# Weight ternarization of a sandwich kernel, issued inside the attention loop instead of behind it

## The chip, the cores and the metric

The kernel runs on one Trainium2 chip, on all 8 of its cores. Each core computes one of the 8 sequences (2048 tokens of 1024 channels) with the whole of the weights, and no core exchanges data with another. The time is that of the device in microseconds (us) for the slowest core.

## What is computed

Two layers, each an attention and a feed-forward part with layer norms around them. Only layer 0 matters here. Cut to what is near the change:

```python
# layer 0, attention
scores = where(tril, (q @ k.T) / sqrt(d), -inf); A = softmax(scores)
out = A @ C - diag(A) * (w2 * v_next)        # C: v convolved over 3 tokens
x = x + layernorm(out)
# layer 0, feed-forward
def _ternary(w):
    scale = maximum(mean(abs(w)), 1e-8)
    return clip(round(w / scale), -1, 1)     # in value
h   = gelu(layernorm(x) @ _ternary(W1).T + b1)
out = h @ _ternary(W2).T + b2
x = x + layernorm(out)
# layer 1 (decay attention, mixture of attention heads and experts): untouched
```

W1 is 4096 x 1024 and W2 1024 x 4096 in fp32, 16 MB each. The ternary weights need a mean over the whole matrix before the first element can be rounded, so each matrix is read twice. They depend on nothing that the attention computes.

## The kernel before

Everything is in one function, `build`. Every engine has one program in order: `kb.q` appends to SyncE's (SP), which issues DMAs, `kb.g` to GpSimd's (POOL), `kb.t` to TensorE's (PE), `kb.v` to VectorE's (DVE), `kb.s` to ScalarE's (ACT). The order of the calls in Python is therefore the order on each engine, and an engine that waits for a semaphore holds up all that was appended to it later. Semaphores `ct`, `cv`, `cs`, `cg` count the work done on PE, DVE, ACT and POOL. A token is a pair of semaphore and count; `wait(engine, *tokens)` waits for each.

The stages around the change, in order:

- **Attention of layer 0** (L515 to L681), 16 query tiles of 128 rows, tile i against the i+1 key tiles before it. Per tile: DVE copies the scores from four PSUM banks to `S_sb` (L565), POOL masks the diagonal block (L572), DVE takes the row maximum (L581), ACT does the exponential into `P_sb` (L587). PE is given the scores of the next tile, `emit_scores(i + 1)` (L547, call at L595), and only behind them the transposes of `P_sb` (L605), which DVE copies to `AT_sb` in one or two batches (L614). DVE then builds `B_sb` and `Dw_sb` (L622, L633), PE transposes `Dw_sb` (L300), DVE copies it (L308), PE forms the output product in `ps_o` (L650, L654), DVE copies that to `q_fm` (L670) and, with POOL, takes the layer norm's sums (`lnb.stats`, L199 to L246). Behind the loop stand `rstd_batch` (Ln and Exp on ACT, L256 and L263) and 16 times `apply` (DVE, L276 to L288).
- **B0, the ternarization** (L684 to L832). Both matrices go by in 32 batches (`batches`) of 128 x 2048 fp32, 1 MB each, through two slots of the buffer `tw`. Pass 1: SP loads a batch (L721) once the slot's last reader is done (`red_tok`), ACT takes the absolute value with a running sum into `asums` (L728). Then a short chain on DVE and PE turns `asums` into the thresholds `taus` (L739 to L782). Pass 2: SP loads the batch again (L804), DVE compares twice (`thr` L811, `wtb` L818), SP stores `wtb` as bf16 to the scratch `w1t_sc` or `w2t_sc` in HBM (L826). The two comparisons and the store share one `thr` and one `wtb`. In SP's program the load of batch k+1 stands behind the store of batch k, which waits for that batch's `wtb`.
- `kb.barrier()` for all engines and DMAs, then a second one without the DMAs.
- **B1** (L840 on): SP loads rows of x (L855), DVE adds the attention's output (L861), layer norm, transposes. Then the feed-forward part of layer 0 reads the ternary weights by transposing DMAs (L919 and w2tb).

Of the kernel before, what the change touches and what calls it, by code (L numbers as in the profile page):

```python
# [6 lines left out]
F32 = mybir.dt.float32  # L7
BF16 = mybir.dt.bfloat16
# [5 lines left out]
D = 1024  # L14
# [62 lines left out]
def wait(eng, *toks):  # L77
    for tk in toks:
        if tk is None:
            continue  # L80
        h, v = tk
        if v > 0:
            eng.wait_ge(h, v)
# [230 lines left out]
def build(debug=(), phases="ABCD"):  # L314
# [194 lines left out]
    kb.flush_dbg()  # L509
    kb.barrier()  # L510

    def outln_ap(i):
        return bass.AP(q_fm, 128 * i, [[q_fm.shape[1], 128], [T, ND], [1, 128]])

    with ExitStack() as pha:  # L515
# [42 lines left out]
        for i in range(NT):  # L558
# [34 lines left out]

            if i + 1 < NT:
                pend = emit_scores(i + 1)  # L595

            at_toks = []
            for bg in range((i + 8) // 8):
# [69 lines left out]
            def _(v, i=i, w=otok):  # L668
# [4 lines left out]

            stok = lnb.stats(outln_ap(i), i, [out_ps_free, rtok],
                             f_ap=ssum[:, 1:2], prev=stok)
        rtok_b = lnb.rstd_batch(0, 16, [stok])
        aptok = None
        for i in range(NT):
# [3 lines left out]
        kb.dbg("outln_q", q_fm[:], a3_done)  # L682
    kb.flush_dbg()

    if "B" in phases:
        NW = 4096 * D
        reg1_free = qkv_done
        NW = 4096 * D
        asums = kb.sbuf("asums", [128, 32], F32)
        taus = kb.sbuf("taus", [128, 4], F32)  # L690
        tot_sb = kb.sbuf("tot_sb", [1, 2], F32)
        ones_f = kb.sbuf("ones_f", [1, 128], F32)
        ones_c = kb.sbuf("ones_c", [128, 1], F32)

        def _(v):
            v.memset(ones_f[:], 1.0)
            cv.inc(v.memset(ones_c[:], 1.0))
        kb.v(_)
        vof = cv.tok()

        W1r = inp["L0_ffn_W1"].rearrange("(c p) d -> p c d", p=128)
        W2r = inp["L0_ffn_W2"].rearrange("(c p) d -> p c d", p=128)
        tw = kb.at("tw", [128, 2 * 2048], F32, REG1)
        thr = kb.at("thr", [128, 2048], BF16, REG1 + 16384)
        wtb = kb.at("wtb", [128, 2048], BF16, REG1 + 20480)
        dts = [kb.dsem("t0"), kb.dsem("t1")]
        red_tok = {0: None, 1: None}
        batches = []
        for b in range(16):
            batches.append((W1r[:, 2 * b:2 * b + 2, :], b))  # L710
        for b in range(16):
            c, h = b // 2, b % 2
            batches.append((W2r[:, c:c + 1, h * 2048:(h + 1) * 2048], 16 + b))
        for src_ap, col in batches:
            slot = col % 2
            twa = tw[:, slot * 2048:(slot + 1) * 2048]

            def _(sync, src_ap=src_ap, twa=twa, w=red_tok[slot], ds=dts[slot],
                  w2=(reg1_free if col < 2 else None)):
                wait(sync, w, w2)  # L720
                ds.inc(sync.dma_start(out=twa.rearrange("p (c d) -> p c d",  # L721
                                                        c=src_ap.shape[1]), in_=src_ap))
            kb.q(_)
            ltok = dts[slot].tok()

            def _(s, twa=twa, col=col, ltok=ltok, pv=red_tok[1 - slot]):
                wait(s, ltok, pv)
                cs.inc(s.activation(thr[:], twa, AF.Abs,  # L728
                                    accum_out=asums[:, col:col + 1]))
            kb.s(_)  # L730
            red_tok[slot] = cs.tok()
        red_all = cs.tok()

        scope_b0 = ExitStack()
        ps_sc = kb.psum("ps_sc", [128, 2], F32, scope_b0)
        for m, (c0, c1) in enumerate(((0, 16), (16, 32))):
            def _(v, m=m, c0=c0, c1=c1, w=red_all):
                wait(v, w)
                cv.inc(v.tensor_reduce(sm[:, 9 + m:10 + m], asums[:, c0:c1], AX.X, ALU.add))  # L739
            kb.v(_)  # L740
        tsum_tok = cv.tok()

        def _(t, w=tsum_tok, w2=vof):
            wait(t, w, w2)
            t.matmul(ps_sc[0:1, 0:1], sm[:, 9:10], ones_c[:], start=True, stop=True)
            ct.inc(t.matmul(ps_sc[0:1, 1:2], sm[:, 10:11], ones_c[:], start=True, stop=True))
        kb.t(_)
        ttot = ct.tok()

        def _(v, w=ttot):  # L750
            wait(v, w)
            cv.inc(v.tensor_scalar_mul(tot_sb[0:1, 0:2], ps_sc[0:1, 0:2], 1.0 / NW))
        kb.v(_)
        vv1 = cv.tok()

        def _(v, w=vv1):
            wait(v, w)
            cv.inc(v.tensor_scalar(tot_sb[0:1, 0:2], tot_sb[0:1, 0:2], 1e-8, 0.5,
                                   ALU.max, ALU.mult))
        kb.v(_)  # L760
        vv2 = cv.tok()

        ps_tau = kb.psum("ps_tau", [128, 2], F32, scope_b0)

        def _(t, w=vv2):
            wait(t, w)
            ct.inc(t.matmul(ps_tau[:, 0:2], ones_f[:], tot_sb[0:1, 0:2],
                            start=True, stop=True))
        kb.t(_)
        tbc = ct.tok()  # L770

        def _(v, w=tbc):
            wait(v, w)
            v.tensor_copy(taus[:, 0:1], ps_tau[:, 0:1])
            v.tensor_copy(taus[:, 2:3], ps_tau[:, 1:2])
            cv.inc(v.tensor_scalar_mul(taus[:, 1:2], ps_tau[:, 0:1], -1.0))
        kb.v(_)
        vt_ = cv.tok()

        def _(v, w=vt_):  # L780
            wait(v, w)
            cv.inc(v.tensor_scalar_mul(taus[:, 3:4], ps_tau[:, 1:2], -1.0))  # L782
        kb.v(_)
        tau_tok = cv.tok()

        W1s = w1t_sc.rearrange("(c p) d -> p c d", p=128)
        W2s = w2t_sc.rearrange("(c p) d -> p c d", p=128)
        dst_sem = kb.dsem("ts")
        st_tok = None
        vthr_tok = None  # L790
        for src_ap, col in batches:
            m = 0 if col < 16 else 1
            slot = col % 2
            twa = tw[:, slot * 2048:(slot + 1) * 2048]
            if col < 16:
                dst = W1s[:, 2 * col:2 * col + 2, :]
            else:
                c, h = (col - 16) // 2, (col - 16) % 2
                dst = W2s[:, c:c + 1, h * 2048:(h + 1) * 2048]

            def _(sync, src_ap=src_ap, twa=twa, w=red_tok[slot], ds=dts[slot],
                  vt=vthr_tok):
                wait(sync, w, vt)
                ds.inc(sync.dma_start(out=twa.rearrange("p (c d) -> p c d",  # L804
                                                        c=src_ap.shape[1]), in_=src_ap))
            kb.q(_)
            ltok = dts[slot].tok()

            def _(v, twa=twa, m=m, ltok=ltok, w=st_tok):
                wait(v, ltok, tau_tok, w)  # L810
                cv.inc(v.tensor_scalar(thr[:], twa, taus[:, 2 * m + 1:2 * m + 2], 1.0,  # L811
                                       ALU.is_ge, ALU.subtract))
            kb.v(_)
            th1 = cv.tok()

            def _(v, twa=twa, m=m, th1=th1):
                wait(v, th1)
                cv.inc(v.scalar_tensor_tensor(wtb[:], twa, taus[:, 2 * m:2 * m + 1],  # L818
                                              thr[:], ALU.is_gt, ALU.add))
            kb.v(_)  # L820
            vthr_tok = cv.tok()
            red_tok[slot] = vthr_tok

            def _(sync, dst=dst, w=vthr_tok):
                wait(sync, w)
                dst_sem.inc(sync.dma_start(  # L826
                    out=dst, in_=wtb[:].rearrange("p (c d) -> p c d", c=dst.shape[1])))
            kb.q(_)
            st_tok = dst_sem.tok()
        kb.barrier()  # L830

        scope_b0.close()  # L832


    kb.barrier(dma=False)


    if "B" in phases:
        scope_b1 = ExitStack()
# [71 lines left out]
        for grp in range(4):  # L911
            for p in range(8):
                slot = p % 2

                def _(sync, p=p, slot=slot, w=w1slot_tok[slot], ds=dw1[slot],
                      w2=(st_tok if (grp == 0 and p < 2) else None)):
                    wait(sync, w, w2)
                    for dc in range(8):
                        ds.inc(sync.dma_start(  # L919
                            out=w1tb[:, slot * 4096 + dc * 512:slot * 4096 + (dc + 1) * 512],  # L920
                            in_=w1t_sc[p * 512:(p + 1) * 512, dc * 128:(dc + 1) * 128],
                            transpose=True))
# [3 lines left out]
                for fpr in range(2):  # L926
# [20 lines left out]
                    kb.t(_)  # L947
                    mtok = ct.tok()

                    def _(s, pb=pb, p=p, fpr=fpr, mtok=mtok, hf=hg_free):  # L950
                        wait(s, mtok, hf)
                        fc0 = 4 * p + 2 * fpr
                        cs.inc(s.activation(h_g[:, fc0 * 512:(fc0 + 2) * 512], pb[:],  # L953
                                            AF.Gelu))
# [8 lines left out]
            for pair in range(2):  # L963
                for fc in range(32):
                    slot = fc % 2
                    wslice = w2tb[:, slot * 1024:(slot + 1) * 1024]
                    def _(sync, fc=fc, wslice=wslice, w=w2slot_tok[slot], ds=dw2[slot],
                          w2=(st_tok if (grp == 0 and pair == 0 and fc < 2) else None)):
                        wait(sync, w, w2)
                        ds.inc(sync.dma_start(out=wslice,  # L970
                                              in_=w2t_sc[:, fc * 128:(fc + 1) * 128],
# [1391 lines left out]
```

How the kernel before makes its waits and increments, by code:

```python
    def inc(self, ins, n=None):  # L67
        n = self.step if n is None else n
        ins.then_inc(self.h, n)
        self.val += n
        return (self.h, self.val)
# [5 lines left out]
def wait(eng, *toks):  # L77
    for tk in toks:
        if tk is None:
            continue
        h, v = tk
        if v > 0:
            eng.wait_ge(h, v)
```

## Time and profile before

| | |
|---|---|
| time, median of 2 runs | 6173.97 us (6172.5 to 6175.44) |
| time of the profiled execution | 6228.01 us |
| its span, core 1 (slowest) | 6226.5 us |
| spans of the 8 cores | 6137.2 to 6226.5 us |
| PE, DVE, ACT, POOL busy | 2947.0, 1919.9, 854.7, 335.0 us |
| chain that ended last | PE 41%, DVE 21%, DMA 14%, issue 9%, ACT 6% |

The profile is of one execution, on its slowest core, core 1; all times below are from that core, counted from its first instruction. The kernel is a sequence of stages with different limits, so that shares over the whole span say little about one stage. In the span, the attention of layer 0 lies at 545 to 953 us, B0 behind it up to 1436 us, B1 up to about 1600 us, and the feed-forward part of layer 0 up to about 2900 us.

### The profile page before, as it was taken

What the parts mean: (1) busy time and instruction counts of PE and PEld (TensorE: products, weight loads), DVE (VectorE), ACT (ScalarE), POOL (GpSimd) and SP (SyncE); (2) the same over time, 40 slices, a digit from 0 to 9 for tenths busy, and PEclk for the clock granted to TensorE, in tenths of its full rate; (3) what the DMA queues carried; (4) which work ended last, traced back from release to release, by engine and by line L of the source; (5) the groups of instructions that cost most, each with busy time, mean ns of one, the idle gap of its engine ahead of it and who ended that gap; (6) DMA issues with size and microseconds to landing.
All of it is one profiled execution on the core that took longest, in us unless ns stands there. A gap on an engine that the chain in (4) does not pass through costs nothing.

```text
span 6226.5 us, 41618 instructions; the slowest of 8 cores (6137.2 to 6226.5 us)
## 1 busy us (share of the span) xinstructions
PE 2947.0 (47%) x11532; PEld 1153.8 (19%) x11532; DVE 1919.9 (31%) x4762; ACT 854.7 (14%) x828; POOL 335.0 (5%) x234
## 2 busy tenths in 40 slices
PE   0672550000666666651342021663432399988970
PEld 0221220000212121210210010221111133333330
DVE  4225441335100000003555642333344222222224
ACT  0000116000204040311000001001100222222220
POOL 2000000001000000001101300000010000000001
PEclk9995775555757575765665555765575678899975
DMA  1100005442343434340001004000000311111102
GB/s 27 27 14 14 0 1 198 153 142 88 68 92 72 95 73 97 73 80 7 0 1 55 0 1 41 0 0 0 14 0 1 54 28 28 28 28 28 28 4 105
DMA packets 494200, 274.39 MB, mean 44 GB/s; under 512 B 439680, under 2 KB 447904, under 8 KB 489888
## 3 DMA queue, kind: packets, MB, share of 16 engines
q1 hardware_dynamic: 438784, 218.18, 13.8%
q0 software_dynamic: 55200, 53.56, 5.6%
q8 instruction: 108, 1.77, 0.1%
q14 instruction: 108, 0.88, 0.1%
HBM read 190.97 MB, written 33.55 MB: 36 GB/s over the span
## 4 chain that ended last, share of the span: by engine, by line
PE 41%; DVE 21%; DMA 14%; issue 9%; ACT 6%; POOL 5%; SPq 2%; DVEq 1%; POOLq 0%; ACTq 0%
DMA w2tb<-w2t_sc 7%; PE ps_m5a L2268 4%; POOL sq_scr L208 4%; DMA tw<-L_ffn_W 4%; PE ps_m5b L2268 4%; PE ps_i5a L2229 4%; PE ps_o L983 4%; PE ps_i5b L2229 4%; PE ps_qkv L441 3%; DVE lnst L214 3%; PE ps_h L937 3%; SPq L919 2%; PE ps_o L650 1%; PE ps_q L1929 1%; PE ps_s L547 1%
## 5 line engine op out<-in xcount | busy, mean ns | idle before, releaser
L983 PE MATMUL ps_o<-w2tb,h_g 128*128 128x512 bf16 x1024 | 439.9, 583 | 277.3 <-DMA w2tb<-w2t_sc 245.8
L937 PE MATMUL ps_h<-act_fm,w1tb 128*128 128x512 bf16 x1024 | 277.9, 420 | 151.5 <-ACT h_g L953 81.1
L2268 PE MATMUL ps_m5a<-w2b,scaled 128*128 128x512 bf16 x1024 | 290.4, 435 | 112.3 <-DVE scaled L2251 112.3
L2241 ACT ACT_TABLE_LOAD x128 | 164.2, 1283 | 843.7 <-PE ps_i5a L2229 755.6
L2268 PE MATMUL ps_m5b<-w2b,scaled 128*128 128x512 bf16 x1024 | 274.8, 417 | 0.0
L2229 PE MATMUL ps_i5a<-act_fm,w1b 128*128 128x512 bf16 x1024 | 248.8, 399 | 28.1 <-DMA w2b<-L_ffn_w 28.1
L208 POOL TENSOR_TENSOR sq_scr<-X 128x1024 f32<-128x1024 f32 x96 | 181.6, 1892 | 1249.6 <-DVE X L861 547.5
L2229 PE MATMUL ps_i5b<-act_fm,w1b 128*128 128x512 bf16 x1024 | 246.9, 397 | 0.0
L2251 DVE TENSOR_TENSOR scaled<-scaled,rw2b_eg 128x512 bf16<-128x512 bf16 x256 | 97.4, 422 | 482.1 <-ACT scaled L2241 482.1
L300 PE MATMUL ps_tr<-idbf,tmb 128*128 128x128 bf16 x128 | 16.2, 305 | 473.9 <-DVE tmb L288 473.9
L1018 DVE TENSOR_REDUCE smB<-out2g 128x1 f32<-128x1024 bf16 x16 | 19.5, 1220 | 711.8 <-ACT out2g L1006 711.8
L256 ACT ACT_TABLE_LOAD x10 | 12.8, 1283 | 1537.5 <-DVE lnst L246 1537.5
L441 PE MATMUL ps_qkv<-n_fm,wbuf 128*128 128x512 bf16 x768 | 184.8, 384 | 78.9 <-DVE q_fm L455 22.7
L983 PEld LDWEIGHTS ps_o<-w2tb,h_g 128*128 128x128 bf16 x1024 | 108.9, 123 | 606.0 <-issue 597.8
L1929 PE MATMUL ps_q<-n1e,qp_b 128*128 128x512 bf16 x256 | 129.0, 504 | 183.5 <-DVE n1e L1914 129.7
L214 DVE TENSOR_REDUCE lnst<-sq_scr 128x1 f32<-128x1024 f32 x144 | 175.7, 1220 | 124.7 <-POOL sq_scr L208 124.7
L300 PE MATMUL ps_trF<-idbf,tmd 128*128 128x128 bf16 x256 | 32.3, 305 | 328.6 <-DVE tmd L288 328.6
L2268 PEld LDWEIGHTS ps_m5a<-w2b,scaled 128*128 128x128 bf16 x1024 | 107.3, 107 | 270.0 <-issue 204.1
L2282 DVE TENSOR_TENSOR X<-X,ps_m5a 128x512 f32<-128x512 f32 x128 | 88.0, 688 | 216.4 <-PE ps_m5a L2268 216.4
L937 PEld LDWEIGHTS ps_h<-act_fm,w1tb 128*128 128x128 bf16 x1024 | 96.8, 104 | 298.1 <-issue 232.7
L547 PE MATMUL ps_s<-k_fm,q_fm 128*128 128x512 bf16 (+3 forms) x320 | 92.1, 464 | 99.0 <-DVE S_sb L565 96.9
L2282 DVE TENSOR_TENSOR X<-X,ps_m5b 128x512 f32<-128x512 f32 x128 | 88.1, 688 | 164.6 <-PE ps_m5b L2268 164.6
(311 smaller groups left out, 4128.4 us busy)
## 6 DMA issues: line engine op xcount, KB each, us to landing
tw<-L_ffn_W SPq DMA_DIRECT2D x64, 1024.0 KB, 5.7
w1b<-L_ffn_w POOLq DMA_DIRECT2D x8, 2048.0 KB, 13.7
w2b<-L_ffn_w POOLq DMA_DIRECT2D x8, 2048.0 KB, 22.7
w1t_sc<-wtb SPq DMA_DIRECT2D x16, 512.0 KB, 3.2
w2t_sc<-wtb SPq DMA_DIRECT2D x16, 512.0 KB, 3.4
xt<-L_attn_x SPq DMA_DIRECT2D x16, 512.0 KB, 3.3
x_sc<-X SPq DMA_DIRECT2D x16, 512.0 KB, 2.6
xt<-x_sc SPq DMA_DIRECT2D x16, 512.0 KB, 4.0
```

The source lines that it names most:

```text
L208: cg.inc(g.tensor_tensor(sq, src_ap, src_ap, ALU.mult))
L214: cv.inc(v.tensor_reduce(va, sq, ax, ALU.add))
L441: t.matmul(pb[:], wbuf[:, slot * 4096 + kc * 512 + fc4 * 128: slot * 4096 + kc * 512 + (fc4 + 1) * 128], n1_fm[:, kc * T + tg * 512: kc * ...
L547: ins = t.matmul(ps_s[bk][:, 0:w1c - w0c], q_fm[:, kc * T + i * 128: kc * T + (i + 1) * 128], k_fm[:, kc * T + w0c: kc * T + w1c], start=( ...
L919: ds.inc(sync.dma_start(out=w1tb[:, slot * 4096 + dc * 512:slot * 4096 + (dc + 1) * 512], in_=w1t_sc[p * 512:(p + 1) * 512, dc * 128:(dc + ...
L937: t.matmul(pb[:, half * 512:(half + 1) * 512], w1tb[:, slot * 4096 + kc * 512 + fl * 128: slot * 4096 + kc * 512 + (fl + 1) * 128], act_fm ...
L983: ins = t.matmul(ps_o2[u][:, half * 512:(half + 1) * 512], h_g[:, fc * 512 + sub * 128:fc * 512 + (sub + 1) * 128], wslice[:, half * 512:( ...
L1929: t.matmul(ps_q3[:], qp_b[:, fl:fl + 128], n1e[:, cc * 512:(cc + 1) * 512], start=st_, stop=sp)
L2229: ins = t.matmul(ps_i5[bk][:, half * 512:(half + 1) * 512], w1b[:, slot * 8192 + cc * 1024 + ic * 128: slot * 8192 + cc * 1024 + (ic + 1) ...
L2241: cs.inc(s.activation(scaled[:, ipr * 1024:(ipr + 1) * 1024], ps_i5[bk][:], AF.Gelu))
L2268: ins = t.matmul(ps_m5[bk][:], scaled[:, ic * 512 + u * 128:ic * 512 + (u + 1) * 128], w2b[:, slot * 8192 + ic * 1024 + half * 512: slot * ...
L2282: cv.inc(v.tensor_add(dd, dd, ps_m5[bk][:]))
```

## The change

The ternarization is cut into steps, closures in a list `b0_steps`: 32 of pass 1, one `tau_step`, 32 of pass 2, 65 in all. The list is made ahead of the attention. In the attention's loop, right behind `emit_scores(i + 1)` and ahead of the transposes of tile i, two steps are taken off and issued in tile 0 and five in each later tile; what is left would be issued behind the loop, ahead of `rstd_batch`. So tiles 0 to 6 get the 32 steps of pass 1, tile 7 gets `tau_step` and four steps of pass 2, tiles 8 to 12 five each, and tile 13 the last three. A step issues on the same engines as before: SP and ACT for pass 1, SP and DVE for pass 2, DVE and PE for tau. The two small PSUM tiles of tau become one of four columns, so that it fits beside the attention's seven banks. The load of pass 2 no longer waits for `vthr_tok`, the batch before; its place in SP's program is the same. The barrier with DMAs behind B0 is gone, the one without stays. The first readers of the scratch and the first writer of the region that `tw` shares with `h_g` wait for the last store and the last comparison.

```diff
+    b0_steps = []
+    b0_state = {}
...
+        def mk_pass1(src_ap, col):
+            def step():
...
+                def _(sync, w=b0_state["red_tok"][slot], ds=dts[slot],
+                      w2=(reg1_free if col < 2 else None)):
+                    wait(sync, w, w2)
+                    ds.inc(sync.dma_start(out=twa.rearrange("p (c d) -> p c d",
+                                                            c=src_ap.shape[1]),
+                                          in_=src_ap))
+                kb.q(_)
+                ltok = dts[slot].tok()
+
+                def _(s, ltok=ltok, pv=b0_state["red_tok"][1 - slot]):
+                    wait(s, ltok, pv)
+                    cs.inc(s.activation(thr[:], twa, AF.Abs,
+                                        accum_out=asums[:, col:col + 1]))
+                kb.s(_)
+                b0_state["red_tok"][slot] = cs.tok()
+            return step
+
+        def tau_step():
+            red_all = cs.tok()
...
+        def mk_pass2(src_ap, col):
+            def step():
...
+                def _(sync, w=b0_state["red_tok"][slot], ds=dts[slot]):
+                    wait(sync, w)
...
+                kb.q(_)
+                ltok = dts[slot].tok()
+
+                def _(v, m=m, ltok=ltok, w=b0_state["st_tok"]):
+                    wait(v, ltok, b0_state["tau_tok"], w)
+                    cv.inc(v.tensor_scalar(thr[:], twa, taus[:, 2 * m + 1:2 * m + 2],
+                                           1.0, ALU.is_ge, ALU.subtract))
+                kb.v(_)
...
+                def _(sync, dst=dst, w=vthr):
+                    wait(sync, w)
+                    dst_sem.inc(sync.dma_start(
+                        out=dst, in_=wtb[:].rearrange("p (c d) -> p c d",
+                                                      c=dst.shape[1])))
+                kb.q(_)
+                b0_state["st_tok"] = dst_sem.tok()
+            return step
+
+        for src_ap, col in batches[:32]:
+            b0_steps.append(mk_pass1(src_ap, col))
+        b0_steps.append(tau_step)
+        for src_ap, col in batches:
+            b0_steps.append(mk_pass2(src_ap, col))
...
             if i + 1 < NT:
                 pend = emit_scores(i + 1)
+            for _k in range(5 if i else 2):
+                if b0_steps:
+                    b0_steps.pop(0)()
...
+        while b0_steps:
+            b0_steps.pop(0)()
         rtok_b = lnb.rstd_batch(0, 16, [stok])
...
+    kb.barrier(dma=False)
     if "B" in phases:
-        NW = 4096 * D
...
-        for src_ap, col in batches:
-            slot = col % 2
...
-        kb.barrier()
-
-        scope_b0.close()
-
-
-    kb.barrier(dma=False)
-
+        scope_b0ps.close()
...
-                    def _(s, pb=pb, p=p, fpr=fpr, mtok=mtok, hf=hg_free):
-                        wait(s, mtok, hf)
+                    def _(s, pb=pb, p=p, fpr=fpr, mtok=mtok, hf=hg_free,
+                          bf=(b0_state.get("st_tok") if grp == 0 and p < 2 else None),
+                          bv=(b0_state.get("vthr_tok") if grp == 0 and p < 2 else None)):
+                        wait(s, mtok, hf, bf, bv)
```

## Rows read from the trace of the kernel before

**Rows 1.** Stages: from:to, length, busy us (instructions) by engine, granted clock, DMA.

```profile
core 1: us, PE busy (x) PEld busy (x) DVE busy (x) ACT busy (x) POOL busy (x), PEclk, DMA share, GB/s
688.00:953.00 265.00, 149.54 (x638) 64.97 (x638) 108.61 (x306) 26.56 (x27) 19.66 (x18) 0.73 0.00 1
957.80:1095.60 137.80, 0.00 (x0) 0.00 (x0) 13.13 (x47) 103.86 (x96) 0.00 (x0) 0.50 0.70 236
1095.60:1435.70 340.10, 0.79 (x6) 0.66 (x6) 117.43 (x72) 0.00 (x0) 0.00 (x0) 0.50 0.43 145
```

**Rows 2.** Tile tw: ns min/median/max, first and last start us; DVE's idle; landing.

```profile
L728 ACT ACTIVATE thr<-tw x32: 1909/1909/1910, 957.8 to 1093.6; 128x2048 bf16<-128x2048 f32 x32
L811 DVE TENSOR_SCALAR thr<-tw,taus x32: 1285/1286/1289, 1098.5 to 1429.4; 128x2048 bf16<-128x2048 f32 x32
...
  DMA tw<-L_ffn_W: 214.9, 31
...
DMA to landing us min/median/max: 4.8/5.7/6.9
```

**Rows 3.** Timeline behind tile 15: start us, us, engine, line, what [idle before].

```profile
953.09 0.16 DVE L246 TENSOR_TENSOR lnst<-lnst 128x1 f32<-128x1 f32 x1
...
956.53 1.28 ACT L728 ACT_TABLE_LOAD   x1
...
957.16 0.55 DVE L288 TENSOR_SCALAR q_fm<-q_fm,lnst 128x1024 bf16<-128x1024 bf16 x1
...
974.92 0.55 DVE L288 TENSOR_SCALAR q_fm<-q_fm,lnst 128x1024 bf16<-128x1024 bf16 x1
```

**Rows 4.** Timeline: tau, the first two batches of pass 2, B1's first load.

```profile
1096.23 0.19 PE L745 MATMUL ps_sc<-ones_c,sm 128*1 128x1 f32 x2 [149.04 <-DVE sm L739]
...
1098.45 1.29 DVE L811 TENSOR_SCALAR thr<-tw,taus 128x2048 bf16<-128x2048 f32 x1
...
1102.28 0.40 SPq L826 DMA_DIRECT2D w1t_sc<-wtb  x1
1102.83 0.37 SPq L804 DMA_DIRECT2D tw<-L_ffn_W  x1
1108.98 1.28 DVE L811 TENSOR_SCALAR thr<-tw,taus 128x2048 bf16<-128x2048 f32 x1 [6.78 <-DMA tw<-L_ffn_W]
1110.38 2.35 DVE L818 SCALAR_TENSOR_TENSOR wtb<-tw,taus,thr 128x2048 bf16<-128x2048 f32 x1
...
1436.10 34.03 SPq L855 DMA_DIRECT2D xt<-L_attn_x  x8
```

**Rows 5.** Timeline of ACT: exponentials of tiles 2, 4, 6, with ACT's idle ahead.

```profile
582.48 1.28 ACT L587 ACT_TABLE_LOAD   x1 [16.47 <-DVE sm L581]
...
622.99 1.28 ACT L587 ACT_TABLE_LOAD   x1 [19.01 <-DVE sm L581]
...
666.85 1.28 ACT L587 ACT_TABLE_LOAD   x1 [19.46 <-DVE sm L581]
```

**Rows 6.** Timeline of DVE: first copies to AT_sb in tiles 7, 8, 13.

```profile
695.58 0.69 DVE L614 COPY AT_sb<-ps_at 128x1024 bf16<-128x1024 bf16 x1 [4.59 <-PE ps_at L605]
...
720.17 0.69 DVE L614 COPY AT_sb<-ps_at 128x1024 bf16<-128x1024 bf16 x1 [4.35 <-PE ps_at L605]
...
865.07 0.69 DVE L614 COPY AT_sb<-ps_at 128x1024 bf16<-128x1024 bf16 x1 [5.64 <-PE ps_at L605]
```

**Rows 7.** Timeline of PE: first half of the output product, tiles 13 and 15.

```profile
871.62 4.55 PE L650 MATMUL ps_o<-C_tm,AT_sb 128*128 128x512 bf16 x14 [1.61 <-DVE ssum L664]
...
936.80 6.50 PE L650 MATMUL ps_o<-C_tm,AT_sb 128*128 128x512 bf16 x16 [1.61 <-DVE ssum L664]
```

**Rows 8.** The page's DMA issues: KB each, us to landing.

```profile
w2b<-L_ffn_w POOLq DMA_DIRECT2D x8, 2048.0 KB, 22.7
...
wbuf<-L_attn_W_qkv POOLq DMA_DIRECT2D x6, 1024.0 KB, 8.6
```

More of the change, by code:

```diff
@@ L683, in build @@
     kb.flush_dbg()
+    kb.barrier(dma=False)
     if "B" in phases:
-        NW = 4096 * D
[L687 to L710, printed above, removed]
@@ L711, in build @@
-        for b in range(16):
-            c, h = b // 2, b % 2
-            batches.append((W2r[:, c:c + 1, h * 2048:(h + 1) * 2048], 16 + b))
-        for src_ap, col in batches:
-            slot = col % 2
[L716 to L829, printed above, removed]
@@ L915, in _ @@
                 def _(sync, p=p, slot=slot, w=w1slot_tok[slot], ds=dw1[slot],
-                      w2=(st_tok if (grp == 0 and p < 2) else None)):
+                      w2=(b0_state.get("st_tok") if (grp == 0 and p < 2) else None)):
                     wait(sync, w, w2)
@@ L967, in _ @@
                     def _(sync, fc=fc, wslice=wslice, w=w2slot_tok[slot], ds=dw2[slot],
-                          w2=(st_tok if (grp == 0 and pair == 0 and fc < 2) else None)):
+                          w2=(b0_state.get("st_tok") if (grp == 0 and pair == 0 and fc < 2) else None)):
                         wait(sync, w, w2)
```

97 lines of the change are left out of this document (added).

## The prediction, written before the changed kernel was run

> **What bounds the kernel now.** I read the page's chain of work that ended last first, to learn that no one engine bounds the whole, then cut the span into stages. The reader is to see two things in [rows 1]. B0 is 137.8 us of pass 1 and 340.1 us of pass 2, and PE does nothing in them (6 instructions in 478 us). The attention ahead of it has no DMA traffic (1 GB/s) and ACT works 26.56 us in 265, so work of the one could lie beside work of the other. Next I read the buffer tw: in pass 2, DVE is idle for 214.9 us in 31 waits, each for a load [rows 2]. The timeline shows why [rows 4]: the store of a batch goes out at 1102.28, the next load right behind it at 1102.83, and DVE begins at 1108.98 after 6.78 us idle. The load is never early, since it stands behind the store on SP, and the store needs the comparisons. So one batch of pass 2 costs a period: (1429.4 - 1098.5) / 31 = 10.67 us [rows 2], of which DVE works 1.29 + 2.35, some 3.7 us with the gap between. Last I read the timeline of the attention: its tiles are one serial chain over DVE, POOL, ACT and PE, in which DVE's idle time is short pieces. This decides the sum: what is put into DVE's program there is hidden only as far as DVE was idle at that very place.
>
> **What is removed.** From the end of tile 15's sums (953.25) to B1's first load (1436.10) is 482.9 us [rows 3, 4]. Of that stretch rstd and the 16 applies stay. They were hidden under pass 1; now their cover is gone, and they end at 975.47, 22.2 us after 953.25 [rows 3]. With 0.3 us for the barrier, 22.5 us stay and 460 us go. B1's first load comes just after the barrier in both kernels, so that its landing costs the same.
>
> **Pass 1 in tiles 0 to 6.** SP's loads wait for nothing but their slots, and SP has nothing else in this stage. On ACT a batch is 103.86 / 32 = 3.25 us busy [rows 1], 3.4 with the gap, and behind the batches stands the next tile's exponential, for which all of the chain waits. Two batches of five have their loads in place when the exponential ends; the others follow at the pace of landing (4.8 to 6.9 us, median 5.7 [rows 2]): starts at about 0, 3.4, 9, 12.5 and 17.5 to 18.5, end at 21 to 22. Between two exponentials ACT was idle 16.47, 19.01 and 19.46 us ahead of tiles 2, 4 and 6 [rows 5]. Against 21 this is late by 4.5, 2.0 and 1.5 us; tiles 3 and 5 I take between, 3 and 2, tile 7 at nothing: 13 us. The bounds: ACT's work alone, 5 x 3.4 = 17, makes it 1 us; the pace of pass 1 of before, (1093.6 - 957.8) / 31 = 4.38 a batch [rows 2] or 22 for five, makes 18. The two batches of tile 0 cost nothing under the idle time ahead of tile 1.
>
> **Tau, in tile 7.** PE reaches it behind the scores of tile 8, which end about 0.7 us before the copy at 695.58 [rows 6]; the chain from its first matmul to pass 2 takes 1098.45 - 1096.23 = 2.2 us [rows 4]. Pass 2 thus begins about 697.1. Its four batches take 3.7 (its load came in long ago) + 3 x 10.67 = 35.7 us, to 732.8: the copy to AT_sb comes 37.3 us late, and PE's transposes are behind tau as well.
>
> **Pass 2 in tiles 8 to 13.** The first load of each tile stands behind the last store of the tile before and is long in place. The other four wait as before, with their order on SP unchanged; the dropped wait for vthr_tok gains nothing, since SP's program holds the load back anyway. DVE is held for 3.7 + 4 x 10.67 = 46.4 us, in tile 13 for 3.7 + 2 x 10.67 = 25.0. Behind it on DVE stands the copy to AT_sb, and for this wait PE's second transposes and the output product, then DVE's own sums and the next tile's scores. What hides is the idle time ahead of that copy, 4.35 to 5.64 us [rows 6]; I take 5 (exponential, scores and first transposes run on under the block). So 5 x 41.4 + 20 = 227 us. With tile 7, pass 2 costs 264 us of its former 340. That is 25 waits for a load where there were 31, and six tiles' gaps of 5 us. A bound from below: nothing of it can take less than the comparisons alone, 32 x 3.7 - 35 = 83 us; from above, with nothing hidden, 300. SP's order speaks for the middle.
>
> **The clock.** PE will be idle some 40 us in each of seven tiles. Now the first half of the output product takes 325 ns a matmul in tile 13 (4.55 / 14), behind recent scores, and 406 in tile 15 (6.50 / 16), which has no scores ahead [rows 7]: the 1.2 GHz level, where 512 columns are 0.43 us, held longer. Like tile 15, tiles 7 to 13 lose 14 x 0.08 = 1.1 us each, 8 in all, and 2 for colder transposes: 10 us. Bounds: nothing, and all 84 matmuls of the second halves at 0.43 in place of 0.21, 18 + 6 = 24 us. The Trainium skill, "TensorE: Matmul & The Clock Gate", section "Part 1: The HAM clock gate (the "warmup" mystery)", says that the slow clock is the default and activity releases it, which speaks against a change that makes PE pause. The trace agrees with the rule in kind (325 against 406 ns). If it were to bite on all of the output products, my sum would be 14 us smaller.
>
> One more rule would speak against mixing Abs and Exp on ACT. In the trace the switch is free: a table load of 1.28 us stands ahead of each batch anyway, and the one at 956.53 comes directly behind an Exp [rows 3]. The Trainium skill, "ScalarE: Activation LUTs", section "What ACT_TABLE_LOAD costs", adds a drain of 1.38 us for a switch to another set; as an estimate that would take 2 x 1.38 us in each of five tiles, 14 us more. The row decides against it.
>
> **Sum.** 460 - 13 - 264 - 10 = 173 us less. Of the profiled execution's 6228 (span 6226.5, 1.5 around it) this leaves 6055. The profiled execution is 54 us above the median of the runs; the stages concerned scarcely hold more than their share of that (attention and B0 are 14% of the span, 8 us), so I carry the difference over whole: 6174 - 173 = 6001 us, 2.8% less.
>
> **The rivals.**
> (a) Dearer loads, within 2%. All eight cores drift apart, and a load may meet others' traffic or work here. It decides from 50 us more (2% of 6174 is 123), 2 us for each of the 25 loads that DVE waits for. At 3 us each, 75 us in all: 6076. Against it: 64 loads of 1 MB landed in 4.8 to 6.9 us with all cores at it, at up to 236 GB/s a core [rows 1, 2], and the new stage asks for less per time. A lesser hiding or a colder PE (10 + 14) push the same way. Chance 0.17.
> (b) Slower. The one mechanism: loads placed in the attention take as long as those that other parts of the kernel show, 8.6 us for 1 MB in wbuf, up to 22.7 for 2 MB in w2b [rows 8], and DVE's block grows with each. Break-even is at 173 / 25 = 7 us more a load, 13 to landing; over 2% slower from 12 us more, about 18. At 22.7 to landing, 17 more: 6001 + 425 = 6426. Those are of POOL's queue with a conversion of type on the way, these are of SP's; nothing of the trace puts SP's above 6.9. Chance 0.04, most of it for slower by over 2%.
> (c) More is hidden. If loads of pass 2 did come ahead of DVE, the block of a tile is 5 x 3.7 = 18.5 less 5 hidden, and the whole 83 + 2 for tau in place of 264: 180 us more saved, 5821. For it: the wait on vthr_tok is gone, and two slots are there. Against it: SP's program order. Chance 0.05.
> (d) The change does not do what it says: the steps only move the wait, and with the applies bare nothing is won. It would need pass 1 to cost on ACT what it did alone, 138 us in place of 13: 6001 + 125 = 6126, within 2%. The idle times of 16 to 19 us a tile speak against it. Chance 0.03.
>
> **How the numbers follow.** The forecast has the remaining 0.71; its own range, from pass 1 (1 to 18), the clock (0 to 24), the hiding (4 to 7 us a tile) and the carry-over to the median, is 5965 to 6040. The range that holds 8 in 10 takes in the nearer part of (a) as well: 5950 to 6070. Faster by over 2% means below 6050: forecast and (c), 0.76; (a) and (d) are within 2%, with part of (b): 0.21; slower 0.03. About 2% is what a measurement of this kernel can tell from no change.
>
> **What would show it.** In the changed kernel's timeline: pass 1's Abs between the exponentials of tiles 0 to 6, and tiles 1 to 5 longer by 1 to 5 us; in tiles 8 to 12 five pairs of comparisons on DVE at 10.5 to 11 us from one to the next, the first without a wait, and each tile some 42 us longer than before; DVE's idle time for loads in pass 2 near 25 x 7 = 175 us in place of 214.9; PE's output products there beginning at over 400 ns a matmul; from the last tile's sums to B1's first load 22 to 23 us; all later stages as long as before. The prediction is wrong if the pairs follow each other at 4 us (c) or at 13 and more (a, b), if exponentials come over 10 us late in tiles 1 to 6 (d), or if a later stage changes its length.

## The result and the profile after

The changed kernel takes 5976.97 to 6020.49 us; its ratio to the kernel before, taken from runs on the same chips, is 0.968 with a 95% interval of 0.962 to 0.974. That is 3.2% less, some 198 us of 6174, where 2.8% and 6001 us were forecast.

The profiled execution of the changed kernel fell on a run in which all eight cores had a lower mean clock (0.677 to 0.687 of full speed, against 0.70 in the runs of 5977 to 5987 us), so its span of 6100.7 us is not to be set against 6226.5. What can be compared is the stretch that the change touches, from the first copy of scores in the attention's tile 0 to B1's first load. On core 1 it is 889.8 us before (546.30 to 1436.10) and 709.4 after (549.07 to 1258.49), 180.4 less; the medians over the eight cores are 888.8 and 710.2.

The stages after on core 1, to be read against [rows 1]: from:to, length, busy us (instructions) of each engine, granted clock, DMA share, GB/s.

```profile
549.10:705.00 155.90, 68.26 (x251) 27.59 (x252) 66.60 (x216) 120.63 (x118) 15.58 (x15) 0.64 0.66 222
705.00:1146.40 441.40, 106.84 (x448) 46.81 (x446) 187.27 (x271) 19.10 (x21) 13.11 (x12) 0.60 0.33 111
1146.40:1236.00 89.60, 44.89 (x189) 19.78 (x189) 35.45 (x106) 6.65 (x6) 6.26 (x5) 0.67 0.02 6
1236.00:1258.50 22.50, 0.00 (x0) 0.00 (x0) 13.95 (x49) 3.09 (x4) 0.00 (x0) 0.50 0.00 0
1258.50:6100.70 4842.20, 2554.04 (x9518) 973.18 (x9518) 1409.05 (x3614) 702.17 (x676) 260.19 (x170) 0.66 0.18 37
```

The first row is tiles 0 to 6 with pass 1: ACT is busy 120.63 of 155.90 us, and the DMA queues run at 222 GB/s beside PE's and DVE's own work. The second, tiles 7 to 13 with pass 2, is the long one: in 441 us DVE is busy 187. The largest part of the rest stands in the answer for the tile tw (min/median/max ns, first and last start; idle us, times), beside [rows 2]:

```profile
L563 ACT ACTIVATE thr<-tw x32: 1909/1910/1911, 556.7 to 701.4; 128x2048 bf16<-128x2048 f32 x32
L645 DVE TENSOR_SCALAR thr<-tw,taus x32: 1276/1286/1287, 710.1 to 1142.8; 128x2048 bf16<-128x2048 f32 x32
...
  DMA tw<-L_ffn_W: 173.1, 25
...
DMA to landing us min/median/max: 4.7/5.8/9.7
```

25 waits for a load, 173.1 us, where the forecast had 25 and near 175. The timeline of tile 8 shows each of them (start us, us, engine, line, what [idle before]), as [rows 4] did before:

```profile
768.98 1.28 DVE L645 TENSOR_SCALAR thr<-tw,taus 128x2048 bf16<-128x2048 f32 x1
...
772.79 0.38 SPq L661 DMA_DIRECT2D w1t_sc<-wtb  x1
773.27 0.42 SPq L637 DMA_DIRECT2D tw<-L_ffn_W  x1
779.09 1.28 DVE L645 TENSOR_SCALAR thr<-tw,taus 128x2048 bf16<-128x2048 f32 x1 [6.37 <-DMA tw<-L_ffn_W]
...
810.81 1.29 DVE L645 TENSOR_SCALAR thr<-tw,taus 128x2048 bf16<-128x2048 f32 x1 [7.05 <-DMA tw<-L_ffn_W]
...
814.47 0.68 DVE L780 COPY AT_sb<-ps_at 128x1024 bf16<-128x1024 bf16 x1
```

The first pair has its load in place, the other four wait 6.4 to 7.1 us, since the load goes out behind the store. The copy to AT_sb, which waited 4.35 us for PE in [rows 6], now waits for nothing and comes 49.1 us after the tile's first copy of scores instead of 8.1.

### The profile page after: what moved, and what is told of

Same layout as the page of the kernel before. It is cut to its first block, busy times and chain, and to the rows that moved or that the text cites. A ratio compares the mean times of both kernels' runs of the same rounds, so it can differ in the third digit from the quotient of the medians.

```text
span 6100.7 us, 41540 instructions; the slowest of 8 cores (6032.4 to 6100.7 us)
## 1 busy us (share of the span) xinstructions
PE 3021.5 (50%) x11532; PEld 1170.2 (19%) x11532; DVE 1918.7 (31%) x4762; ACT 854.7 (14%) x828; POOL 335.0 (5%) x234
## 3 DMA queue, kind: packets, MB, share of 16 engines
q1 hardware_dynamic: 438784, 218.18, 13.9%
## 4 chain that ended last, share of the span: by engine, by line
PE 42%; DVE 22%; DMA 13%; issue 9%; ACT 6%; POOL 5%; SPq 2%; DVEq 1%; POOLq 0%; ACTq 0%
DMA w2tb<-w2t_sc 7%; PE ps_m5a L2289 5%; POOL sq_scr L208 4%; PE ps_m5b L2289 4%; PE ps_i5a L2250 4%; PE ps_i5b L2250 4%; PE ps_o L1004 4%; DMA tw<-L_ffn_W 3%; PE ps_qkv L441 3%; PE ps_h L956 3%; DVE lnst L214 3%; SPq L938 2%; PE ps_q L1950 1%; DVE n1e L1935 1%; PE ps_o L816 1%
## 5 line engine op out<-in xcount | busy, mean ns | idle before, releaser
L956 PE MATMUL ps_h<-act_fm,w1tb 128*128 128x512 bf16 x1024 | 295.6, 441 | 142.5 <-ACT h_g L974 79.1
L2250 PE MATMUL ps_i5a<-act_fm,w1b 128*128 128x512 bf16 x1024 | 257.5, 410 | 22.9 <-DMA w2b<-L_ffn_w 22.9
L1039 DVE TENSOR_REDUCE smB<-out2g 128x1 f32<-128x1024 bf16 x16 | 19.5, 1220 | 727.9 <-ACT out2g L1027 727.9
L750 ACT ACT_TABLE_LOAD x16 | 20.5, 1283 | 924.8 <-DVE sm L744 924.7
L771 PE MATMUL ps_at<-idbf,P_sb 128*128 128x128 bf16 x136 | 13.8, 247 | 259.8 <-DVE AT_sb L780 233.0
## 6 DMA issues: line engine op xcount, KB each, us to landing
w1b<-L_ffn_w POOLq DMA_DIRECT2D x8, 2048.0 KB, 13.5
w2b<-L_ffn_w POOLq DMA_DIRECT2D x8, 2048.0 KB, 22.6
```

Source lines behind the costliest of these rows:

```text
L956: t.matmul(pb[:, half * 512:(half + 1) * 512], w1tb[:, slot * 4096 + kc * 512 + fl * 128: slot * 4096 + kc * 512 + (fl + 1) * 128], act_fm ...
L2250: ins = t.matmul(ps_i5[bk][:, half * 512:(half + 1) * 512], w1b[:, slot * 8192 + cc * 1024 + ic * 128: slot * 8192 + cc * 1024 + (ic + 1) ...
```

## The experiments

Each was run beside the kernel before on the same chip. The figure that decides is the stretch, as the median over the eight cores; the ratio stands beside it.

| kernel | attention begins | stretch | later stages | ratio to before (95%) |
|---|---|---|---|---|
| before | 547.3 | 888.8 | 4731.6 | 1 |
| changed | 548.0 | 710.2 | 4800.4 | 0.968 (0.962 to 0.974) |
| e1, pass 1 alone in the loop | 548.6 | 778.2 | 4712.4 | 0.982 (0.967 to 0.996) |
| e2, dropped wait put back | 548.5 | 711.2 | 4708.9 | 0.969 (0.960 to 0.979) |
| e3, loads ahead of the store | 548.5 | 625.5 | 4733.4 | 0.955 (0.948 to 0.963) |
| e4, and two wtb | 548.4 | 585.0 | 4754.2 | 0.950 (0.940 to 0.959) |
| e5, steps at two places | 548.0 | 505.9 | 4716.5 | 0.935 (0.930 to 0.941) |
| e6, ahead of the attention | 534.2 | 430.4 | 4735.9 | 0.923 (0.918 to 0.928) |
| e7, four banks alone | 477.2 | 715.4 | 4733.6 | 0.959 (0.954 to 0.963) |
| e9, spread over both | 497.9 | 431.2 | 4705.1 | 0.913 (0.897 to 0.930) |

**The theory**: DVE's program in order is the cost. Pass 2 costs its full period in the attention, less DVE's short idle time at that place, and the period is long because the load stands behind the store on SP. **The rivals**: pass 1 or a later stage is the gain; the dropped wait is; the landing or the queues' bandwidth sets the period, not the order.

**e1.** Pass 2 is taken out of the loop:

```diff
-                if b0_steps:
+                if len(b0_steps) > 33:
                     b0_steps.pop(0)()
```

> Only pass 1 is issued inside the attention's loop; tau and pass 2 stand behind the loop, ahead of rstd. Measured from the first score copy of tile 0 to B1's first load, the kernel before takes 889.8 us and the changed one 709.4. Theory (the sum of the prediction, step by step): pass 1 hides all but 10 us, tau and pass 2 cost 343 as before, rstd and the applies are bare: 407 + 10 + 343 + 22.5 = 782 us, 107 less than before, 73 more than the changed kernel; ratio to the kernel before about 0.983. Rival (pass 1 was the whole gain and moving pass 2 brought nothing): 710 us, ratio as the changed kernel's, 0.968. Rival (pass 1 hides poorly, pass 2 well): above 830 us, ratio over 0.99.

Measured 778.2 us, 4 off. So of the change's 179 us, pass 1 brings 111 and pass 2 68, though pass 2 is the longer by far (340 against 138). In ACT's idle time pass 1 is hidden but for some 10 us; what else is missing from 138 is mostly the 22.6 us of rstd and applies, which it used to cover. Pass 2 is mostly moved. The interval of its ratio is wide, 0.967 to 0.996; the stretch carries the verdict.

**e2.** The wait that the change drops is put back:

```diff
-                def _(sync, w=b0_state["red_tok"][slot], ds=dts[slot]):
-                    wait(sync, w)
+                def _(sync, w=b0_state["red_tok"][slot], ds=dts[slot],
+                      vt=b0_state["vthr_tok"]):
+                    wait(sync, w, vt)
```

> The changed kernel with the one dropped wait put back: SP's load of pass 2 waits again for the comparisons of the batch before. Theory (the order of SP's program holds the load back anyway, the dropped wait is worth nothing): no difference, 709 us for the stretch, 25 waits for loads of about 7 us, 173 us in all, ratio 0.968 to the kernel before. Rival (part of the gain came from this wait): pairs of comparisons further apart than the 10.5 of the changed kernel, stretch over 720 us.

711.2 against 710.2 us, and 25 waits, 176.9 us in all, on the profiled core. The wait was worth nothing: the load stands behind a store that waits for the same comparisons.

**e3.** The load of batch k+2 is issued behind the store of batch k, so that the one of k+1 is out before:

```diff
-                def _(sync, w=b0_state["red_tok"][slot], ds=dts[slot]):
-                    wait(sync, w)
...
+                if col == 0:
+                    load2(0)
+                    load2(1)
+                ltok = b0_state["ltok"][col]
...
                 b0_state["st_tok"] = dst_sem.tok()
+                if col + 2 < 32:
+                    load2(col + 2)
```

> The changed kernel with one thing moved: in pass 2 the load of batch k+2 is issued behind the store of batch k, so that the load of batch k+1 is always ahead of that store. Theory (SP's program order is what DVE pays for): DVE no longer waits for loads; the next limit is the one wtb, whose store has to land, 3.7 + about 3.8 us = 7.5 from one pair to the next; the block of five is 34 us in place of 46, and 25 x 3.1 = 78 us go: stretch 631 us, ratio to before about 0.956. Rival (the queues cannot carry load and store together, or the landing is what is slow): pairs stay 10 us or more apart, stretch above 690 us.

625.5 us, and the waits changed their name as expected. Timeline of DVE and SP, then the waits of the tile tw in this kernel:

```profile
799.84 1.28 DVE L656 TENSOR_SCALAR thr<-tw,taus 128x2048 bf16<-128x2048 f32 x1 [3.30 <-DMA w1t_sc<-wtb]
801.23 2.35 DVE L663 SCALAR_TENSOR_TENSOR wtb<-tw,taus,thr 128x2048 bf16<-128x2048 f32 x1
803.65 0.38 SPq L672 DMA_DIRECT2D w1t_sc<-wtb  x1
804.12 0.42 SPq L632 DMA_DIRECT2D tw<-L_ffn_W  x1
```

```profile
  DMA w1t_sc<-wtb: 44.1, 13
  DMA w2t_sc<-wtb: 43.3, 12
```

DVE waits for the store of its single wtb, 3.3 us each, and never for a load; the pairs are 7.1 us apart in place of the 10.3 to 10.8 above. Nothing but the order on SP was changed, and the loads land no faster (5.9 us at the median over pass 2, 6.0 in the changed kernel). So it was the order that put the load's landing into each period; a limit of bandwidth would have kept the pairs 10 us apart.

**e4.** The kernel of e3, and with two wtb, each with a semaphore for its store (a part of the edit, against the changed kernel):

```diff
-        wtb = kb.at("wtb", [128, 2048], BF16, REG1 + 20480)
-        dst_sem = kb.dsem("ts")
+        wtb2 = kb.at("wtb", [128, 2 * 2048], BF16, REG1 + 20480)
+        dsts = [kb.dsem("ts0"), kb.dsem("ts1")]
...
-                def _(v, m=m, th1=th1):
-                    wait(v, th1)
...
+                def _(v, m=m, th1=th1, w=b0_state["st"][slot]):
+                    wait(v, th1, w)
```

> As the one before, and with two wtb buffers, each with its store semaphore. Theory: the store's landing goes off the path too; of five batches in a tile two find their loads in place, the others come at the pace of landing, one load being issued each time a slot is read: the block is about 23 us, in tile 7 17 and in tile 13 13: some 149 us less than the changed kernel, stretch 560 us, ratio to before about 0.945. Rival (1 MB in and 0.5 MB out per batch saturate the queues): pairs 8 us or more apart, stretch above 620 us, no better than with the one buffer.

585.0 us: 125 less than the changed kernel, not the 149 expected, and between the theory's 560 and the rival's 620. The waits for loads are back, 54.7 us in 17, and the landings are longer than reckoned: from 697 us on, that is over pass 2, 7.6 us at the median and 10.9 at most, where the changed kernel has 6.0 and 8.0. In tile 9 a load issued at 809.59 is read at 817.52:

```profile
809.59 0.42 SPq L632 DMA_DIRECT2D tw<-L_ffn_W  x1
...
812.44 1.29 DVE L659 TENSOR_SCALAR thr<-tw,taus 128x2048 bf16<-128x2048 f32 x1 [3.39 <-DMA tw<-L_ffn_W]
...
817.52 1.28 DVE L659 TENSOR_SCALAR thr<-tw,taus 128x2048 bf16<-128x2048 f32 x1 [1.27 <-DMA tw<-L_ffn_W]
```

**e8.** To tell what made these landings long, e4 with the stores in the loop cut to 16 columns (`out=dst[:, 0:1, 0:16], in_=wtb[:, 0:16]`), and full stores, all from one buffer, behind the loop (so the ternary weights that it stores are not the right ones):

> As e4_two_out, but in the loop each store of pass 2 is cut to 16 columns, 4 KB; the stores in full stand behind the loop, all from one buffer, so the ternary weights of this kernel are wrong and about 80 us of stores come on top behind the loop. It tells why the block of five in e4_two_out is 25.6 us and not the 23 expected. Theory (loads are slowed by the 0.5 MB stores that run beside them): with the stores gone the loads that DVE waits for land in 5 to 5.7 us in place of 6.8 to 7.9, and the block is 22.5 to 23 us. Rival (two loads in flight slow each other, or the wait is SP's): landing and block stay as in e4_two_out, 25 us or more.

The waits for loads fall to 28.1 us in 15 from 54.7 in 17:

```profile
  DMA tw<-L_ffn_W: 28.1, 15
```

Over pass 2 its loads land in 5.2 us at the median and 6.3 at most, with two of them in flight as in e4, so two loads do not slow each other by much. From the first comparison to the copy to AT_sb, tiles 8 to 12 take 22.9 to 25.0 us on the profiled core, in e4 25.6 to 31.9; from tile 7's first copy of scores to that of tile 14 the medians over the cores are 321.5 and 344.0 us. The full stores beside the loads thus cost about 23 us, and e4 lay 25 above its 560: they are nearly all of its excess. (The stretch of e8, 565.5 us, holds the added stores behind the loop and is not set against the others.)

**e5.** In the kernel of e4, from tile 7 on one step stays at its place (in tile 7 tau and one) and three go behind the output product's matmuls:

```diff
-            for _k in range(5 if i else 2):
+            for _k in range(2 if i == 0 else (5 if i < 7 else (2 if i == 7 else 1))):
                 if b0_steps:
                     b0_steps.pop(0)()
...
             at_free = otok
+            for _k in range(0 if i < 7 else 3):
+                if b0_steps:
+                    b0_steps.pop(0)()
```

> As e4_two_out, but from tile 7 on four steps a tile at two places of DVE's program: one (in tile 7 tau and one) where the changed kernel has its steps, three behind the output product's matmuls, where DVE was idle 7.5 to 10.8 us for PE. Pass 2 then ends in tile 14. Theory (what is put into DVE's program is hidden only as far as DVE was idle at that place): the first step is covered, the three cost 12 us of comparisons and 3 of a wait for a load against 7.5 to 10.8, so 5 to 7 us a tile: the stretch from the first score copy to B1's first load goes from 585 (median of the cores, e4_two_out) to about 505 us, ratio to before about 0.937. Rival (the tiles are paced by the DMA queues, 6 MB a tile, wherever the steps stand): no better than 570.

505.9 us, for 505 expected. The same instructions, at other places of the same program, cost 79 us less. Not all of this is idle time used: the steps are also further apart, and DVE's waits for loads fall by 23 us (on core 5, from 54.7 in 17 to 31.8 in 8). Some 56 us are left for the place alone. The timeline of DVE in tile 11:

```profile
865.10 0.69 DVE L797 COPY AT_sb<-ps_at 128x1024 bf16<-128x1024 bf16 x1 [1.51 <-PE ps_at L788]
...
882.44 1.29 DVE L659 TENSOR_SCALAR thr<-tw,taus 128x2048 bf16<-128x2048 f32 x1 [3.75 <-DMA tw<-L_ffn_W]
883.90 2.35 DVE L666 SCALAR_TENSOR_TENSOR wtb<-tw,taus,thr 128x2048 bf16<-128x2048 f32 x1 [0.17 <-DVE thr L659]
886.24 1.21 DVE L856 CAST q_fm<-ps_o 128x1024 bf16<-128x1024 f32 x1
```

The copy to AT_sb still waits 1.51 us for PE, so the single step ahead of it cost nothing. The copy of the output comes 21.1 us behind it, 13.5 before: the three steps overrun PE's work by 7.7, half of it a wait for the third load.

**e6, e7.** The whole ternarization goes ahead of the attention, with its buffers where C_tm comes later: a step of pass 1 behind each tile of the first layer norm and beside the first groups of the projection, tau behind group 8, pass 2 over groups 9 to 95. The projection gets four PSUM banks in turn; e7 is the changed kernel with only this:

```diff
-                bk = fc4 % 2
-                pb = ps_q[bk]
                 for tg in range(4):
+                    bk = tg
+                    pb = ps_q[bk]
```

> The whole ternarization is moved ahead of the attention: pass 1 beside the first layer norm and the first groups of the q, k, v projection (SP and ACT idle there), tau and pass 2 beside the rest of the projection, one batch every 2.7 of its 96 groups, loads two ahead, two wtb, buffers in the region of C_tm. The projection gets four PSUM banks in turn in place of two. Theory: the attention and what follows go back to 407 + 23 = 430 us for the stretch (888.8 before, 710.2 changed, medians of the cores); the projection's DVE has 66 us of its own and gets 120 in 283, mostly hidden with four banks, so that the attention begins at 480 to 520 us (548 before); in all some 310 us less than the changed kernel, ratio to before about 0.915. Rival (DVE's blocks of 3.7 us stall PE in the projection in spite of the banks): the attention begins at 580 or later, ratio 0.93 or more.

> The changed kernel with the four banks in turn in the q, k, v projection alone, to tell their part in e6_early. Theory: PE no longer waits for DVE's copy between groups (68 us of idle time in the projection), the attention begins at about 480 us in place of 548, stretch unchanged at 710, ratio to before about 0.958. Rival: PE is bound by its own issue and weight loads, under 20 us are won.

The stretch is 430.4 us in e6, what the attention, rstd and applies took by themselves (407 + 23): everything of B0 is off it. e7 begins its attention at 477.2 us: the banks alone are worth 71 us, a gain that has nothing to do with the change. Against e7, e6 begins 57 us late, more than the 3 to 43 expected, and its ratio is 0.923 where 0.915 was expected.

**e9.** Tau behind group 20, 20 batches of pass 2 beside the projection, 12 one each in tiles 3 to 14:

> As e6_early, but tau stands behind group 20 of the projection's 96 instead of 8 (PE waited 24 us for pass 1 there), only 20 batches of pass 2 go beside the projection, one every 3.75 groups, and the last 12 go one each into the attention's tiles 3 to 14, at the changed kernel's place, with buffers in the region of n1_fm. Theory (e6_early lost its 57 us at the attention's start to tau and to loads: 1.5 MB a batch want 6.4 us and got 5.8): the attention begins at 485 to 495 us (534 in e6_early, 477 in e7_banks), the single steps in the tiles have their load in place and lie in DVE's idle time of 2.4 to 5.6 us, about 1 us each or less uncovered: stretch 430 to 442 us; some 40 us less than e6_early, ratio to before about 0.916. Rival (the projection loses by DVE's blocks themselves, 3.7 us against PE's two or three groups of lead): the start stays over 515 us.

Start 497.9, stretch 431.2 us, ratio 0.913: the lowest of all, though its interval is wide, 0.897 to 0.930, and holds that of e6. The profiles tell the two apart: start and stretch together are 929 us, some 35 less than in e6. The twelve single steps in the attention cost 1 us together against e6: a pair of 3.7 us lies in the idle time in front of AT_sb. The rival falls: the 20 batches beside the projection waited 1.0 us for loads in all, and none of PE's waits for DVE in it is over 0.7 us (tau apart). Still the start is 21 us behind e7's and 3 behind what was expected. Part of it is the projection's own first load: on core 1, PE begins the projection at 193.24, in e7 at 176.98. The timeline of e9 (core 1), then the landing of wbuf's six loads:

```profile
170.33 1.79 POOL L611 DMA_DIRECT2D wbuf<-L_attn_W_qkv  x2 [63.77 <-DVE n_fm L308]
...
193.24 3.57 PE L630 MATMUL ps_qkv<-n_fm,wbuf 128*128 128x512 bf16 x8 [25.07 <-DMA tw<-L_ffn_W]
```

```profile
DMA to landing us min/median/max: 8.2/18.4/29.5
```

PE waits 25.07 us, which the trace puts down to a load of tw; but its wait there is for wbuf, whose load went out at 170.33. In e7 the same wait is 13.9 us. With the ternarization's loads in flight, wbuf's take 18.4 us at the median (21.9 in e6) in place of the 8.6 of [rows 8]; they are POOL's and convert fp32 to bf16. e6's 57 us were followed only in part: on core 1 its projection begins at 187.27, 10 us behind e7's, and PE waited 19.5 us for DVE's copies in it, as the rival had it; the rest stays open.

## Why the prediction was right, point by point

Against the steps of the prediction, on core 1:

| step | forecast | measured |
|---|---|---|
| stretch removed, rstd and applies left | 482.9, 22.5 | 482.9, 22.6 |
| pass 1 in tiles 0 to 6 | 13 (1 to 18) | 10.3 |
| tau and four batches in tile 7 | 37.3 | 39.0 |
| pass 2 in tiles 8 to 13 | 227 | 225.0 |
| colder PE | 10 (0 to 24) | 5.3 |
| net | 173 | 180.4 |

**The bare applies.** From the end of tile 15's sums to B1's first load, the changed kernel's timeline, as [rows 3] before:

```profile
1235.93 0.16 DVE L246 TENSOR_TENSOR lnst<-lnst 128x1 f32<-128x1 f32 x1
...
1240.00 0.55 DVE L288 TENSOR_SCALAR q_fm<-q_fm,lnst 128x1024 bf16<-128x1024 bf16 x1
...
1258.49 0.80 SPq L874 DMA_DIRECT2D xt<-L_attn_x  x2
```

**Pass 1.** ACT's timeline, tiles 2, 4 and 6, beside [rows 5]:

```profile
590.06 1.28 ACT L750 ACT_TABLE_LOAD   x1
...
592.08 1.28 ACT L563 ACT_TABLE_LOAD   x1
...
635.02 1.28 ACT L750 ACT_TABLE_LOAD   x1
...
680.49 1.28 ACT L750 ACT_TABLE_LOAD   x1
```

These exponentials wait for nothing but ACT itself, as forecast: ACT was late there, not DVE. The attention begins 2.8 us later than before; net of that, tile 2's exponential comes 4.8 us late (590.06 - 582.48 - 2.77), and by tile 7 the delay is 10.3 us. The forecast's pace of landing, 21 us for five, was right in tile 1 (568.78 to 590.06, 21.3 us) and a little high later: in tile 4 five batches took 20.5. The switch between Exp and Abs cost its table load of 1.28 us, which stands ahead of every batch, and nothing else, as the row had it: the load for the next Abs begins at 592.08, and tile 2's exponential ends at 592.06. The drain that the Trainium skill, "ScalarE: Activation LUTs", section "What ACT_TABLE_LOAD costs", adds for a switch to another set does not show here. By its section "Table sets: the hidden batching unit" it was not to be expected: abs is in every set, so Exp to Abs is no switch to another one, and the prediction's 14 us did not apply. The trace agrees; it does not tell what a real switch of sets costs.

**Tile 7.** The batches were as reckoned except for two: the first load behind tau's landed in 8.0 us and was waited for 8.8, the next was waited for 7.4. The longest wait but this one is 8.5 us in tile 12, for a load that landed in 7.4 (the 9.7 of the tile tw's answer is a load of pass 1 in tile 0). Before, no load took over 6.9 us to land. So loads can be dearer under the attention, but few were: the mean of DVE's waits is 6.9 us, as before (173.1 / 25 and 214.9 / 31). Rival (a) needed 2 us more on each of 25.

**Pass 2 in tiles 8 to 13.** The delays of the copy to AT_sb were 41.1, 40.5, 40.6, 41.3, 42.8 and 18.8 us, for 41.4 five times and 20 forecast; the 42.8 of tile 12 has the slow load just named. This step carried the forecast, and e2 and e3 show two of its premises: the dropped wait did nothing, and SP's order made the period. e5 bears out the third, that the place in DVE's program decides what is hidden, with 56 of its 79 us.

**The clock.** Right in sign, half as large. From the copy to AT_sb to that of the output, tiles 7 to 13 take 5.3 us more in all. In tile 13 the first half of the output product, beside [rows 7]:

```profile
1153.52 4.98 PE L816 MATMUL ps_o<-C_tm,AT_sb 128*128 128x512 bf16 x14 [1.61 <-DVE ssum L830]
```

It takes 356 ns a matmul, between the 325 of tile 13 and the 406 of tile 15 before. The granted clock over these matmuls is 0.63 here, and was 0.69 in tile 13 and 0.55 in tile 15: the clock rose to its 2.4 GHz level earlier in this half than in tile 15. The likeness to tile 15 is what the term had wrong. It was also summed too high: a half has as many matmuls as the tile has key tiles, 8 in tile 7 up to 14 in tile 13, 77 in all and not 7 times 14, which makes 6 us of its 8. The Trainium skill, "TensorE: Matmul & The Clock Gate", section "Part 1: The HAM clock gate (the "warmup" mystery)", has the slow clock as the default that activity releases; the trace agrees in kind, with 0.63 granted where 0.69 was.

**The whole.** The forecast 6001 us is 173 less than 6174; the stretch's median gave 178.6. The measured ratio stands for 198 us, with an interval of some 36 to either side, and the difference to the stretch is within it. Whatever it is would lie in the stages behind B1's first load, the same program in both kernels but for the waits on the last store and comparison: in the ten profiled kernels of the table they take 4705 to 4800 us. By the prediction's own sign of being wrong, a later stage that changes its length, the changed kernel's profile is 69 us off there (4800.4 against 4731.6). But e2, the same kernel but for a wait that did nothing, takes 4708.9, and in the changed kernel's profile PE is busy 2554.04 us with the same 9518 matmuls that took 2485.47 before. So these stages scatter by more than what is left to explain, and not by the change. What sets PE's clock in them was not examined, and that the difference carries over whole from the profiled execution to the median was assumed and not tested.

Rival (c), more hidden, needed loads ahead of the stores: e3 and e4 made just this and got 85 and 125 us of its 180. Rival (d) needed pass 1 to stay bare: in e1 it brings 111 us of its 138.

## What to carry to other kernels

Work moved into another stage is hidden only against the idle time of its engine at that place of that engine's program, and an engine in order brings its waits along: count waits, not busy time. Before moving a loop, look at what its period is made of; here two thirds of it were a wait that came from the order of two DMAs in SP's program, and mending that (e3, 85 us) was worth more than moving the loop was (68 us for pass 2). No run mends the order with pass 2 left behind the attention. As an estimate, 31 periods of 7.1 in place of 10.67 us would bring e1's 778 us down to about 668, so that moving pass 2 as well (e3, 625.5) would then be worth some 42 us. And a stage in which the engines of the moved work have room is a better host than one where they stand on the critical chain with short gaps: beside the first layer norm and the projection, with four banks, the whole ternarization cost 57 us of start in e6 and left the stretch at the attention's own 430 us; spread over both places (e9) it cost 21 and 1.

## What the runs showed of the hardware

- Loads of 1 MB on SP's queue, over pass 2 (min, median, max to landing): 5.4, 6.0, 8.0 us in the changed kernel; 5.2, 7.6, 10.9 in e4, with two loads and two 0.5 MB stores in flight; 4.9, 5.2, 6.3 in e8, where the stores are cut to 4 KB. DVE's waits for them fell from 54.7 us in e4 to 28.1 in e8.
- The 1 MB loads of wbuf, POOL's and with conversion, lose far more: 8.6 us at the median (15.0 at most) without SP's loads beside them, 18.4 (29.5) in e9 and 21.9 (32.6) in e6 with them, while SP's own loads went from 5.7 to 6.5 us in e9.
- A switch between Exp and Abs on ACT cost the 1.28 us table load that stands ahead of each of these activations anyway: exponential's end at 592.06, table load at 592.08.
